# A two-layer attention and expert kernel: in the first attention, the scores move to the head of TensorE's step and the first two transposes of probabilities stand in a row

## What is computed

```
q = _split_heads(query @ Wq.T + bq)          # 16 heads of 16
k = _split_heads(key @ Wk.T + bk)
v = _split_heads(value @ Wv.T + bv)
scores = jnp.einsum('bhqd,bhkd->bhqk', q, k) / SCALE
scores = jnp.where(attn_mask == 0, jnp.float32(-1000000000.0), scores)
w = jax.nn.softmax(scores, axis=-1)
att = jnp.einsum('bhqk,bhkd->bhqd', w, v)
x = att + key                                # then layer norm, gamma, beta
```

## Time and profile before

| | us |
|---|---|
| Median of 3 runs | 966.21 |
| Lowest and highest run | 964.13, 966.92 |
| The profiled execution | 958.49 |
| Its span, from the first to the last instruction | 956.6 |
| TensorE busy in the span | 864.7 (90%) |
| VectorE, ScalarE, GpSimd busy | 595.3, 467.7, 381.6 |

### The profile page before, as it was taken

The page is one execution under the profiler, slowest core; times in us unless marked ns, Lnnn a source line. Parts: engine busy times, 40 slices in busy tenths (PEclk is TensorE's granted clock), DMA queues, the critical chain, the costliest instruction groups (busy, mean ns, idle before and its releaser), DMA issues. The chain is left out here.

```text
span 956.6 us, 26657 instructions
## 1 busy us (share of the span) xinstructions
PE 864.7 (90%) x9044; PEld 731.3 (76%) x9045; DVE 595.3 (62%) x1484; ACT 467.7 (49%) x1194; POOL 381.6 (40%) x610
## 2 busy tenths in 40 slices
PE   5888888779999999997999899999999999689995
PEld 4676776549999999986566688888888887568784
DVE  3587887555545555542027476878678778459995
ACT  3788787422222222222343455445545454359894
POOL 4478887620000000007101346445555453436652
PEclk9999999789999999999999999999999999889997
DMA  6445656352333333316864597677687866212211
GB/s 167 131 153 164 188 164 213 130 209 70 119 96 108 95 99 95 96 39 204 291 204 149 140 186 170 144 158 177 138 170 138 176 134 124 62 35 64 66 52 46
DMA packets 190188, 128.27 MB, mean 134 GB/s; under 512 B 128545, under 2 KB 175649, under 8 KB 189985
## 3 DMA queue, kind: packets, MB, share of 16 engines
q1 hardware_dynamic: 155728, 93.72, 38.3%
q10 hardware_dynamic: 31312, 25.17, 9.3%
q0 software_dynamic: 3072, 8.39, 2.7%
HBM read 78.25 MB, written 48.99 MB: 133 GB/s over the span
## 5 line engine op out<-in xcount | busy, mean ns | idle before, releaser
L1763 ACT ACTIVATE c_pT<-c_T 128x512 f32<-128x512 f32 (+2 forms) x90 | 50.2, 595 | 101.9 <-PE c_T L1925 71.5
L1706 POOL TENSOR_TENSOR c_soft<-c_soft,c_share 128x616 f32<-128x616 f32 (+2 forms) x96 | 70.4, 762 | 60.6 <-DVE c_share L2181 59.0
L1094 ACT ACTIVATE b_rowsT<-b_RT 128x256 f32<-128x256 f32 x39 | 15.0, 385 | 152.8 <-PE b_RT L1136 152.8
L1716 POOL MEMSET d_round<- 128x1 f32 x1 | 0.1, 98 | 222.1 <-POOLq L981 222.1
L1145 PE MATMUL b_U<-b_rowsT,b_w 128*128 128x128 f32 x624 | 76.7, 277 | 0.0
L1222 DVE SCALAR_TENSOR_TENSOR b_hidT<-b_U,b_bias,b_gate 128x128 f32<-128x128 f32 x156 | 43.9, 344 | 52.5 <-PE b_U L1145 52.5
L1172 PE MATMUL b_Y<-moe_w,b_hidT 128*128 x312 | 73.9, 380 | 0.9 <-DVE b_out L1255 0.9
L1145 PEld LDWEIGHTS b_U<-b_rowsT,b_w 128*128 128x128 f32 x624 | 73.5, 194 | 0.0
L516 ACT ACTIVATE early<-a_S,early 128x128 f32<-128x128 f32 x256 | 70.7, 433 | 3.7 <-DVE early L796 3.7
L2039 PE MATMUL c_O<-early,c_attT 128*128 128x256 f32 x256 | 61.7, 396 | 5.0 <-ACT c_attT L1837 4.4
L1975 PE MATMUL c_T<-c_xT,early 128*128 128x128 f32 x512 | 61.0, 277 | 3.4 <-ACT c_kT L1763 2.4
(11 more groups left out here) (245 smaller groups left out, 2143.1 us busy)
## 6 DMA issues: line engine op xcount, KB each, us to landing
moe_w<-in_L_Wl SPq DMA_DIRECT2D x16, 512.0 KB
rel_windows<-c_relw ACTq DMA_DIRECT2D x28, 276.0 KB, 5.6
c_bias<-rel_windows SPq DMA_DIRECT2D x16, 462.0 KB, 5.0
prob_rows<-c_soft SPq DMA_DIRECT2D x16, 462.0 KB, 5.5
early<-in_L_early SPq DMA_DIRECT2D x16, 384.0 KB, 3.2
values<-c_pT ACTq DMA_DIRECT2D x22, 256.0 KB, 2.7
first_rows<-expert_lists SPq DMA_DIRECT2D x39, 128.0 KB, 2.6
expert_out<-b_out SPq DMA_DIRECT2D x39, 128.0 KB, 1.7
```

What stands on the lines that cost most here:

```text
L1706: ins = nc.gpsimd.tensor_tensor(soft[p][:, hs, a:z], soft[p][:, hs, a:z], share[:, s, hs].unsqueeze(2).to_broadcast([P, HS, z - a]), ALU.mult)
L1763: nc.scalar.activation(dst, view(T[k]), ACT.Copy, **kw).then_inc(g["emptied"], 1)
```

## The change

In TensorE's `steps`, the call of `scores(b)` moves from behind the first transpose of probabilities to the head of the step, ahead of `attention(b - 2)` and `places(b - 4)`. The first and the second transposes of probabilities, which stood on either side of it, now follow each other. No instruction is added or taken away, the other engines' queues are as they were, and every wait stays with its call.

```
 def steps(b, i, p):
+    if there(b):
+        scores(b, p)
     if there(b - 2):
         attention(b - 2)
     if there(b - 4):
         places(b - 4, p)
     if there(b - 1):
         probabilities(b - 1, 1 - p, 0)
-    if there(b):
-        scores(b, p)
-    if there(b - 1):
         probabilities(b - 1, 1 - p, 1)
     if there(b - 3):
         next_rows(b - 3, 1 - p)
```

5 lines of the change are left out of this document (2 added, 3 removed).

## The result

| | before | after |
|---|---|---|
| Median in this comparison | 965.17 (4 runs, 959.15 to 966.92) | 952.12 (4 runs, 950.78 to 953.46) |
| Ratio, 95% interval | | 0.9886 [0.9851, 0.9921] |
| The profiled execution, its span | 958.49, 956.6 | 953.46, 951.6 |

The change makes the kernel faster, by about 11 us by the ratio and 13 by the medians. I had forecast 6.3 and a time of 959.9; 952.12 lies under the range of 957.2 to 965.0. The two profiled executions differ by only 5.0 us, which is less than the forecast. Both facts have to be explained.

What follows compares the result with a forecast made beforehand. The first attention's step was taken to be bound by a ring of waits, no engine full. Twelve steps at 0.40 give 4.8, steps 1 to 3 give 1.5, sum 6.3: 966.2 to 959.9 us, range 957.2 to 965.0.

Steps and rivals of the forecast that it cites:

- The ring: Attention step of 10.19 us, counted from E, the last exponential's end: waits among engines, TensorE idle 1.21 ahead of `attention`; saving 0.55.
- The first path through VectorE: `denominators` waits for `attention`, so VectorE's chain to the maxima moves 0.70; exponentials at E+5.07 at best, saving 0.35.
- rival (c): Slower: scores ahead of `attention` wait for VectorE's keys (line 787), delayed through GpSimd; 967.8, up to 971; chance 0.08.
- The cap: GpSimd's turn, 9.66 us of own work and gaps, limits a step's saving to 0.53; mean with 0.39 is 0.46, taken 0.40.
- 0.35 + (0.86 - d): Saving per step with d the duration of VectorE's line 845: 0.53 at the median 0.675, 0.39 at 0.82.
- The lock: Skill's rule for VectorE and GpSimd's port pair: no saving in steps where line 845 comes just behind line 429's start.
- Rival (d): Line 845 stands in each step until line 429 is done, 1.28 us; only 1.5 saved, 964.7; chance 0.04.
- rival (a): VectorE keeps the pace, line 845 meeting the residuals every step at 0.96; 0.25 saved a step, 961.7; chance 0.12.
- The first steps: Steps 1 to 3 of the first attention, with less or no other work: 0.5 us saved each, 1.5 in all.
- Carried to the end: The whole 6.3 us reaches the next stage; TensorE's 3.54 us wait hides VectorE and GpSimd ending up to 1 us later.
- Rival (e): Steps shorten, but the way into the experts' stage or TensorE's lower clock gives it back; 966.2; chance 0.11.
- The step that failed: Profiled execution lies 7.7 us under the median; saving taken as the same there, so 966.2 - 6.3 = 959.9.

Runs made afterwards that it cites:

- the third trace of before: Kernel before, no edit, profiled in a later set beside the kernel after: 960.03 us (12 runs), ratio 1.0025 against the same kernel.
- the row only: Kernel before with the first two transposes of probabilities in a row, scores still behind the attention: 958.54 us (10 runs), ratio 0.9952.
- the loads behind: Kernel before with the loads of the experts' weights issued behind the steps instead of in them: 994.33 us, ratio 1.0331.
- the execution of 965.51 us with clean steps: Profiled execution of kernel before, scatters writing 8 numbers of a row instead of 256, experts reading input rows: 959.76 us (12 runs), ratio 1.0000.
- the second trace of the kernel before: Kernel before, no edit, run and profiled once more: 962.55 us (10 runs), ratio 1.0003; span of the profiled execution 962.6.

## Why the prediction was wrong

**The ring, right.** The wait that I named was the one, and the terms came as worked out: scores just behind E, first copy at E+2.55 (forecast 2.51), exponentials at E+5.11 (5.0 to 5.1), 117.95 us from step 3 to step 15 (117.8). The first path through VectorE holds, as line 671 waits for 844 (0.24 in the row above), and line 787 (786 after) delays only line 590, by 0.37; rival (c) fell.

**The cap, wrong in kind, not in size.** I averaged 0.53 from GpSimd's 9.66 with 0.39. The run without line 429 shows that the length of GpSimd's turn doesn't bind. What is left is the path over line 844: it takes 0.70 in the median of its sixteen instances in the kernel after, where I took 0.675, and waits 0.17 for line 416. By 0.35 + (0.86 - d) that would be 0.51 less the wait, 0.34; measured 0.385. GpSimd sets the pace after all, but through its lines 416 and 428, as follows.

**The lock, right in kind, wrong in its price.** Rival (d) wanted line 845 to stand until GpSimd's addition is done, and I put that at 0.40 + 0.88 = 1.28 and gave it a chance of 0.04, since none took more than 0.96. The rows say that it does stand. In the earlier trace rows line 845 goes from 95.55 to 96.41. GpSimd beside it, kernel before:

```profile
95.53 0.73 POOL L429 TENSOR_TENSOR early<-early 128x256 f32<-128x256 f32 x1
```

This ends at 96.26, 0.15 ahead. Over the twenty traces line 845, or its like, runs 320 times. 58 times it has neither of the two additions beside it and takes 0.32 to 0.41 us. 241 times it ends 0.15 to 0.17 behind the end of one, whatever was left of that addition, and 21 times it starts in the last 0.22 us of one and takes 0.32 to 0.40. It works the other way too: the 0.88 of line 429 in the earlier trace rows is one beside which line 845 had started 0.11 earlier and took 0.40; undisturbed, line 429 takes 0.73. So the one that comes second stands until the other is done, and of line 845 only 0.15 us are left then, not 0.40. In the kernel after, line 844 stands so for line 428 in nine of the eleven full steps: 0.70 in the median instead of 0.40, or 0.3 us in a step. So rival (a) was right that the two engines' phases are locked to each other, with 0.70 in place of its 0.96. That is why leaving out line 429 changed nothing there. The Trainium skill, page "SBUF — State Buffer", section "SBUF: two separate sides", tells of an exclusive lock for the whole of the other's instruction, for VectorE in a two-port mode; this trace agrees with the lock, and whether the line runs in such a mode no run shows.

**The first steps, right in the mean.** I gave 0.5 each to steps 1 to 3. Steps 2 and 3 saved 1.0 together; step 1 lost 0.9 in the profiled execution, at the lower clock, and took 9.73 and 9.87 in the other two against 10.06 and, in the third trace of before, 28.16 - 18.05 = 10.11. Step 1 and the stage together take 4.7, 6.5 and 6.2 us less in the three traces of the kernel after than in the clean ones of the kernel before; 6.3 was forecast.

**Carried to the end, right.** Rival (e) fell: 5.16 us are there at line 664 of the earlier trace rows and 5.06 at the start of the next stage.

**The step that failed** is this one: "It is 7.7 under the median for reasons that the trace doesn't show, and I take the saving to be the same." The profiled execution had no late copies, and the runs around it very likely had. In the kernel before they come in some executions: in the one that was traced the twelve steps take 128.80 us instead of 122.57, and 5.5 of the 6.2 us are left at the end of the stage. The new order has had none in five traces with scatters (the result's, two more, step 1 in the old order, and without line 429). What the difference between an execution and its median hides is not always neutral to a change. Here it was about half of the gain.

How much of this is shown: in the traces, that late copies exist, that they fall beside the scatters and cost 5.5 us in one execution, and that the ring by itself saves 5.6 to 6.2. In the times, that the kernel before has two levels 5 us apart at like clock, that the kernel after has one, and that without the scatters 7.5 us are gone in a set of the upper level. That every run of the upper level has late copies is inferred from three traces, one of it and one each with the row only and with the loads behind. For the result's own set it is inferred too, since no run at 965 was traced there and no clock is on record; as the execution of 965.51 us with clean steps shows, the later stages alone can add up to 7 us. That the new order escapes because its copies lie ahead of the second scatter is argued: they still fall beside the first one. Why an execution has late copies or not stays open.

## What to carry to other kernels

When the profiled execution lies well under the median, the difference is itself a row that is missing: take a second profile before pricing a change, and look in it for instructions that start late though what they wait for is done. Compare runs of like granted clock before calling two medians different. A ring of waits is won by moving work into the idle time ahead of its bottleneck; here each position that I gave for the step came out within 0.1 us of the forecast. When an instruction's length varies, set its end beside the ends of the other engines' instructions: here that shows at once that line 845 was standing and for what. And an order is perhaps also worth what it keeps out of each other's way: the last waits of ScalarE now lie ahead of GpSimd's second scatter.

## What the runs showed of the hardware that I had not expected

- TensorE's signal to ScalarE can come up to 1 us after TensorE is done (ScalarE idle 0.92 and 1.02 in the second trace of the kernel before), while GpSimd is at an indirect scatter. The copy then mostly starts 0.34 to 0.52 us behind the second scatter's end, once 0.16 behind it and a few times ahead of it. It comes in long series, eight steps in a row in one trace, and in other executions of the same kernel not at all. The Trainium skill, page "SBUF — State Buffer", section "SBUF: two separate sides", names only the port pair of VectorE and GpSimd as shared; whether any port plays a part here no run shows, as the time is lost ahead of the copy. What sets the one or the other is open; the loads of the experts' weights are not needed for it, and neither bytes nor issuing could be tested, since their sets had none.
- A VectorE instruction of 0.40 us (line 845) and a GpSimd addition on 128x256 elements stand for each other: VectorE's ends 0.15 us behind the addition's end, in 241 of 320 instances.
- GpSimd once stood still for 4.92 us ahead of its first indirect scatter.
- The same sixteen matmuls of the scores in step 1 took 1.03, 1.14, 1.28 or 1.92 us in different executions, by the granted clock at that moment (0.50 in the execution with 1.92).
